# Attention with two passes over the scores: PSUM banks handled in units of two

## The reference

```python
h = _layernorm(x) * (1 + ca) + sa
q, k, v = split(h @ qkv_w + qkv_b)             # 16 heads of 8
q, k = _apply_rotary(q, rope), _apply_rotary(k, rope)
scores = einsum('bhqd,bhkd->bhqk', q, k) * 8 ** -0.5
scores = where(causal_mask, -inf, scores)
x = x + ga * (softmax(scores) @ v @ out_w + out_b)
h = _layernorm(x) * (1 + cb) + sb
x = x + gb * ffn(h)                            # routed expert: h = leaky(x @ w_fc) ** 2, h @ w_proj
```

## Time and profile before

| | |
|---|---|
| median of 3 runs | 369.53 us |
| the runs | 368.46 to 371.78 us |
| span of the profiled execution | 368.0 us |
| busy: TensorE, VectorE, ScalarE, GpSimd | 340.0, 258.0, 208.2, 103.8 us |

### The profile page before, as it was taken

How to read it: one execution, slowest core, us unless ns; L and a number is a source line. 1 busy time by engine, 2 the same in 40 slices (tenths; PEclk the granted TensorE clock), 3 DMA queues, 4 the chain that set the end, 5 groups by cost and what they waited for, 6 DMA issues and landing times.

```text
span 368.0 us, 6868 instructions
## 1 busy us (share of the span) xinstructions
PE 340.0 (92%) x2332; PEld 160.5 (44%) x2360; DVE 258.0 (70%) x563; ACT 208.2 (57%) x399; POOL 103.8 (28%) x189
## 2 busy tenths in 40 slices
PE   6999789999799898999999989999999999899886
PEld 4545345443354432443543434344434445434555
DVE  4947667987999977587667878677887777423254
ACT  5350056754166666677356665864666665785341
POOL 3543253427410424401301212101204232443221
PEclk9999889999999999999899999999999999999999
DMA  6547512221410003340230500500000000000000
GB/s 202 184 118 189 139 44 69 67 67 25 113 44 0 3 1 73 74 101 0 67 89 6 130 2 2 131 1 30 1 2 3 3 3 1 4 0 3 28 2 29
DMA packets 13314, 18.87 MB, mean 51 GB/s; under 512 B 4192, under 2 KB 9184, under 8 KB 13280
## 3 DMA queue, kind: packets, MB, share of 16 engines
q1 hardware_dynamic: 12992, 18.04, 18.4%
q10 hardware_dynamic: 288, 0.39, 0.3%
HBM read 12.98 MB, written 5.24 MB: 50 GB/s over the span
## 4 chain that ended last, share of the span: by engine, by line
PE 67%; issue 9%; DVE 8%; POOL 3%; ACT 2%; DMA 0%; SPq 0%; ACTq 0%; POOLq 0%; DVEq 0%
PE ps_o L1066 18%; PE ps L1029 15%; PE ps L1046 13%; PE ps L1000 4%; PE ps L987 4%; DVE tmax L864 3%; PE ps L936 3%; PE ps L1024 2%; DVE rot L760 1%; PE ps L1008 1%; PE ps L993 1%; PE ps L927 1%; PE ps L940 1%; ACT pt L660 1%; PE ps L947 1%
## 5 line engine op out<-in xcount | busy, mean ns | idle before, releaser
L864 DVE TENSOR_REDUCE tmax<-ps 128x1 f32<-128x512 f32 (+3 forms) x304 | 186.4, 656 | 65.4 <-PE ps L1029 65.0
L660 ACT ACTIVATE pt<-ps 128x512 f32<-128x512 f32 (+1 forms) x304 | 161.9, 576 | 105.6 <-PE ps L1046 104.1
L1029 PE MATMUL ps<-kst,qst 72*128 72x128 bf16 (+3 forms) x576 | 113.9, 274 | 3.6 <-issue 2.2
L1046 PE MATMUL ps<-qst,kst 75*128 75x512 bf16 (+3 forms) x384 | 111.0, 327 | 4.9 <-DVE rot L760 1.8
L1066 PE MATMUL ps_o<-pt,v_sb 128*32 128x512 f32 (+3 forms) x768 | 83.5, 507 | 2.0 <-ACT pt L660 1.1
L1029 PEld LDWEIGHTS ps<-kst,qst 72*128 72x128 bf16 x576 | 49.1, 98 | 70.0 <-ACT pt L660 17.9
L556 POOL TENSOR_SCALAR_AFFINE_SELECT pt<-pt 128x512 f32<-128x512 f32 x64 | 40.4, 641 | 68.0 <-ACT pt L660 67.5
L1046 PEld LDWEIGHTS ps<-qst,kst 75*128 75x128 bf16 x384 | 34.9, 98 | 29.6 <-issue 6.4
L1008 PE MATMUL ps<-maska,identb 128*128 128x512 bf16 x118 | 34.1, 396 | 3.5 <-POOL maska L483 3.3
L521 POOL CAST negp<-negm 128x16 bf16<-128x16 f32 x16 | 3.2, 198 | 94.4 <-DVE negm L781 94.2
L1066 PEld LDWEIGHTS ps_o<-pt,v_sb 128*32 128x32 f32 x768 | 15.5, 108 | 32.2 <-issue 17.3
(11 more groups left out here) (102 smaller groups left out, 250.8 us busy)
## 6 DMA issues: line engine op xcount, KB each, us to landing
qst<-qparts SPq DMA_DIRECT2D x48, 96.0 KB
kst<-kparts SPq DMA_DIRECT2D x48, 96.0 KB
qparts<-part SPq DMA_DIRECT2D x16, 96.0 KB, 1.9
kparts<-part SPq DMA_DIRECT2D x16, 96.0 KB, 1.9
xs<-in_x SPq DMA_DIRECT2D x4, 256.0 KB, 7.2
rope_sb<-in_rope SPq DMA_DIRECT2D x2, 512.0 KB, 6.2
qparts<-part SPq DMA_DIRECT2D x16, 64.0 KB, 1.8
qst<-negt SPq DMA_DIRECT2D x48, 4.0 KB, 1.7
```

The lines of the kernel that those rows point to most:

```text
L660: act.activation(pt[:, G % NP, h0:h0 + nh, 0:w], src, ACT.Exp, scale=SCALE).then_inc(s_exp, 1)
L864: dve.tensor_reduce(dst, src, AX.X, ALU.max).then_inc(s_max, 1)
L1029: last = pe.matmul(dst[:, j * nk:(j + 1) * nk], qst[0:ROWS, half, h, r * P:r * P + P], kst[0:ROWS, kh, h, k0:k0 + nk], start=(kind != "dia ...
L1046: last = pe.matmul(dst[:, j * w:(j + 1) * w], kst[:, kh, h, kt * P:kt * P + P], qst[:, half, h, c0:HALF], start=True, stop=True)
```

## The change

Pass A hands its banks over in units of up to two of one kind, and pass B in units of up to two of one group. Both diagonal blocks of two neighbouring rows make a unit (the second of them moves ahead of the tri and sq banks of its row), the tri block with a single bank stays alone, and so does a B group with one bank. A unit stands at the slot of its first bank and covers the following slot too. TensorE fills both its banks one after the other and signals once, after the last matmul. In a slot it now does the B unit first, then the A unit; `uses` has the same order. VectorE reduces, and ScalarE takes the exponential of, a whole unit in one instruction where its two banks are neighbours in the ring; where the ring ends between them (bank 6, then bank 0) there are two instructions. `bank_free` waits for the instruction that reads the bank in question. LEAD, PVLAG, NB and the stages' slots are as before.

```diff
-def bank_jobs_a(half):
+def bank_units_a(half):
+    units = []
     for r in range(TU):
-        jobs.append(("diag", r, 0, HG, P))
+        if r % 2 == 0:
+            units.append(("diag", [(r, 0), (r + 1, 0)], HG, P))
         if r:
             nh = min(HG, HALF // (r * P)) if r < 3 else 1
-            jobs += [("tri", r, h, nh, r * P) for h in range(0, HG, nh)]
+            banks = [(r, h) for h in range(0, HG, nh)]
+            units += [("tri", banks[j:j + 2], nh, r * P) for j in range(0, len(banks), 2)]
         if half:
-            jobs += [("sq", r, h, 1, HALF) for h in range(HG)]
+            units += [("sq", [(r, h), (r, h + 1)], 1, HALF) for h in range(0, HG, 2)]
...
+UNIT_B = 2
+NB = 7
...
         for gi, grp in enumerate(groups_b(half)):
-            for bank in grp[3]:
-                b_at[slot] = (s, gi, grp, bank, bank is grp[3][-1])
-                slot += 1
+            for j in range(0, len(grp[3]), UNIT_B):
+                unit = grp[3][j:j + UNIT_B]
+                b_at[slot] = (s, gi, grp, unit, unit[-1] is grp[3][-1])
+                slot += len(unit)
...
     for i in range(slots):
-        uses += [("a", i)] if i in a_at else []
-        uses += [("b", i)] if i in b_at else []
+        uses += [("b", (i, j)) for j in range(len(b_at[i][3]))] if i in b_at else []
+        uses += [("a", (i, j)) for j in range(len(a_at[i][1][1]))] if i in a_at else []
...
+    def operations(kind, i, n):
+        at = [use_no[(kind, (i, j))] % NB for j in range(n)]
+        return [(0, n)] if at == list(range(at[0], at[0] + n)) else [(j, 1) for j in range(n)]
...
             def exp(i):
-                act.wait_ge(s_b, n + 1)
+                act.wait_ge(s_b, unit_b[i] + 1)
...
-                src = bank_of("b", i)[:, 0:nh * w].rearrange("p (h q) -> p h q", h=nh)
-                act.activation(pt[:, G % NP, h0:h0 + nh, 0:w], src, ACT.Exp, scale=SCALE).then_inc(s_exp, 1)
+                for j, n in exp_ops[i]:
+                    h0, nh = unit[j]
+                    b0 = use_no[("b", (i, j))] % NB
+                    src = ps[:, b0:b0 + n, 0:nh * w].rearrange("p b (h q) -> p b h q", h=nh)
+                    dst = pt[:, G % NP, h0:h0 + n * nh, 0:w].rearrange("p (b h) q -> p b h q", b=n)
+                    act.activation(dst, src, ACT.Exp, scale=SCALE).then_inc(s_exp, 1)
...
-                    dve.wait_ge(s_a, i + 1)
+                    dve.wait_ge(s_a, unit_a[i] + 1)
...
+                    for j, n in max_ops[i]:
+                        r, h0 = banks[j]
+                        b0 = use_no[("a", (i, j))] % NB
+                        src = ps[:, b0:b0 + n, 0:nh * nk].rearrange("p b (h k) -> p b h k", h=nh)
...
+                        dve.tensor_reduce(dst, src, AX.X, ALU.max).then_inc(s_max, 1)
...
                 if kind == "a":
-                    pe.wait_ge(s_max, which + 1)
+                    pe.wait_ge(s_max, n_max[which])
                 if kind == "b":
-                    pe.wait_ge(s_exp, bank_no[which] + 1)
+                    pe.wait_ge(s_exp, n_exp[which])
...
+                for n, (r, h0) in enumerate(banks):
+                    dst = take("a", (i, n))
...
                 last.then_inc(s_a, 1)
...
             for i in range(slots):
+                if i in b_at:
+                    pass_b(i)
                 if i in a_at:
                     pass_a(i)
-                if i in b_at:
-                    pass_b(i)
-                if i not in b_at and i < max(a_at):
+                if i not in b_slots and i < a_end[-1] - 1:
                     keep_warm(1)
```

More of the change, by code:

```diff
@@ L122, in plan @@
     for s, (b, half, g) in enumerate(STEPS):
-        for job in bank_jobs_a(half):
-            a_at[n] = (s, job)
-            n += 1
+        for unit in bank_units_a(half):
+            a_at[n] = (s, unit)
+            n += len(unit[1])
         a_end.append(n)
@@ L186, in plan @@
                     at = put(at, name, (b, half, piece))
-    slots = max(list(a_at) + list(b_at) + list(v_at) + list(stages)) + 1
+    slots = max(a_end[-1:] + list(b_at) + list(v_at) + list(stages)) + 1
     return slots, a_at, b_at, v_at, stages, a_end
@@ L202, in adaln_block @@
         group_no.setdefault(b_at[i][0:2], len(group_no))
-    bank_no = {i: n for n, i in enumerate(sorted(b_at))}
+    unit_a = {i: n for n, i in enumerate(sorted(a_at))}
+    unit_b = {i: n for n, i in enumerate(sorted(b_at))}
+    b_slots = {i + j for i in b_at for j in range(len(b_at[i][3]))}
     prep_no = {u: n for n, u in enumerate(PREPS)}
@@ L294, in adaln_block @@
         y = sb("y", [P, TU, D])
-        NB = 7
         ps = bank("ps", NB)
@@ L1016, in pass_a @@
             def pass_a(i):
-                s, (kind, r, h0, nh, nk) = a_at[i]
+                s, (kind, banks, nh, nk) = a_at[i]
                 b, half, g = STEPS[s]
-                if i == 0 or a_at[i - 1][0] != s:
+                if i == 0 or a_end[s - 1] == i:
                     stack_ready(s)
-                dst = take("a", i)
-                if kind == "diag":
-                    pe.matmul(dst, identb[:, :], maska[:, :, :].rearrange("p h k -> p (h k)"), start=True, stop=False,
-                              skip_group_check=True)
@@ L1026, in pass_a @@
-                for j in range(nh):
-                    h = HG * g + h0 + j
-                    k0, kh = (r * P, half) if kind == "diag" else (0, half) if kind == "tri" else (0, 0)
-                    last = pe.matmul(dst[:, j * nk:(j + 1) * nk], qst[0:ROWS, half, h, r * P:r * P + P],
-                                     kst[0:ROWS, kh, h, k0:k0 + nk], start=(kind != "diag"), stop=True,
-                                     skip_group_check=True)
+                for n, (r, h0) in enumerate(banks):
+                    dst = take("a", (i, n))
+                    if kind == "diag":
+                        pe.matmul(dst, identb[:, :], maska[:, :, :].rearrange("p h k -> p (h k)"), start=True, stop=False,
+                                  skip_group_check=True)
+                    for j in range(nh):
+                        h = HG * g + h0 + j
+                        k0, kh = (r * P, half) if kind == "diag" else (0, half) if kind == "tri" else (0, 0)
+                        last = pe.matmul(dst[:, j * nk:(j + 1) * nk], qst[0:ROWS, half, h, r * P:r * P + P],
+                                         kst[0:ROWS, kh, h, k0:k0 + nk], start=(kind != "diag"), stop=True,
+                                         skip_group_check=True)
@@ L1042, in pass_b @@
                     pe.wait_ge(s_mstack[s % 2], 48 * (s // 2 + 1))
-                dst = take("b", i)
-                for j in range(nh):
-                    h = HG * g + h0 + j
-                    last = pe.matmul(dst[:, j * w:(j + 1) * w], kst[:, kh, h, kt * P:kt * P + P],
-                                     qst[:, half, h, c0:HALF], start=True, stop=True)
+                for n, (h0, nh) in enumerate(unit):
+                    dst = take("b", (i, n))
+                    for j in range(nh):
+                        h = HG * g + h0 + j
+                        last = pe.matmul(dst[:, j * w:(j + 1) * w], kst[:, kh, h, kt * P:kt * P + P],
+                                         qst[:, half, h, c0:HALF], start=True, stop=True)
@@ L1088, in _ @@
                     run(st)
-                    if i > max(b_at) and st[0] in WARM_POST:
+                    if i > max(b_slots) and st[0] in WARM_POST:
                         if st[0] == "n3" or st[1] == last_piece(len(UNITS) - 1):
```

45 lines of the change are left out of this document (28 added, 17 removed).

## The result

The changed kernel takes 397.99 us (median of 4 runs, 397.90 to 398.58) against 370.65 us (368.46 to 373.67) of the kernel before: a ratio of 1.076, interval [1.072, 1.0801], slower by 27 us. The forecast was 377 us and a range of 365 to 387. The direction came out, the size did not.

The account below looks back on a forecast made before the run. TensorE was taken to set the pace outside crowded stretches. Holes of 10.9 us, less 1.1 and 1.0, plus 0.3, gave 9.1, taken as 8; added to 369.5 this made 377.5, stated as 377 us, range 365 to 387.

Parts of the forecast that it names:

- The merged operations: Merged reductions on VectorE and exponentials on ScalarE: 8.4 and 11.6 us less busy time, 1.0 us counted on the path.
- The holes of the ring: TensorE waits 0.38 us before the V product for a bank that a merged reduction frees late.
- the list: Slots 79 to 303, where both passes run: 33 places short of TensorE work, 10.9 us together.
- net term: Holes of 10.9 us, less 1.1 and 1.0 for the crowded stretch, plus 0.3 in the tail: 9.1 us.
- the last part of the sum: VectorE's and ScalarE's other work ahead of awaited units, left out: 33 places at 0.2 more would be 6.6 us.
- Other parts: TensorE's instructions unchanged in number and size, B before A only reorders banks; 0.3 us in the tail, bounds 0 and 1.
- Slots before 79 at nothing: Single-pass slots before 79 counted as costing nothing, covered by a warming matmul per slot or the V product.
- a lost cover: Before slot 79, if warming matmuls or V products no longer cover the waits: up to 4.7 us.
- The clock: A drop of the granted clock, 1.00 in the quiet stretches, would spoil the reckoning upward; no size given.
- Piled-up holes: Rival, 386 us, chance 0.13: VectorE's stages ahead of merged reductions make 33 holes grow by 0.2 to 0.4 us.
- Balance: Rival, 370 us, chance 0.23: half the holes or less are new, 3 to 5 us, met by readers' savings of 3.
- faster: Rival, 364 us, chance 0.17: VectorE bounds more than one stretch, 5 to 6 of its saved 8.4 us come through.

Follow-up runs that it names:

- e17: Changed kernel's TensorE order, banks signalled one by one, merged reads moved to the slot of the unit's last bank, behind the first slot's stages; 376.74 us.
- e10: Changed kernel's TensorE order, but every bank signalled and read by itself at its own slot, nothing merged; 371.70 us.
- e14: Changed kernel with ten filling matmuls ahead of the first B unit and nine ahead of the first transposition of the maxima; 396.57 us.
- e6: Changed kernel with ten filling matmuls ahead of the first B unit; 397.41 us.
- e9: Kernel before with ten and five filling matmuls ahead of the first two transpositions of the maxima; 370.93 us.
- e15: Kernel before with ten filling matmuls ahead of the first transposition of the maxima and ten ahead of the first B bank; 370.69 us.

## Why the prediction was wrong, point by point

**The merged operations** were right: 1,220 and 1,023 ns against 1,215 and 1,018, and 120 and 129 fewer of them. VectorE's busy time fell by 6.2 us and ScalarE's by 11.4, for 8.4 and 11.6. None of it reached the end of the run. The Trainium skill (Perfetto Trace Analysis, section Optimizing Scalar/DVE Operations) says that instructions may better be broken up where Scalar and Vector are not saturated but make bubbles elsewhere; e17 against e10 agrees, 7.1 us longer in the middle for fewer operations.

**The holes of the ring** were right in place and mechanism, 0.40 for 0.38 us, and nearly so in number: e17 has 24 places and 8.4 us in the middle where the list had 33 and 10.9 us over a somewhat longer stretch; 6 of the 24, with 1.9 us, stand in e10 too. Their net term, 9.1 us, measured 7.1 in the middle of e17 and some 5 us in its whole time over e10.

**The step that failed** is the last part of the sum: "What VectorE's and ScalarE's other work adds when it stands ahead of a unit that TensorE waits for is not in it". First, it was left out of the sum, with 6.6 us as the most. Second, only one direction was seen, a stage that makes a unit late. The other direction decided: a unit that stands ahead of a stage makes the stage late by its wait for the second bank and its longer read, 0.75 us at the place shown, and TensorE waits for the stage's bank. Between the changed kernel and e17, which differ in this, in GpSimd's mask at the last bank's slot, and in the units that the ring splits (e17 signals and reads them bank by bank), lie 398.0 - 376.7 = 21 us. Some of that goes with the clock; with it nearly equal, e14 against e17 (8.2 and 2.2 us at 1.2 GHz there), the steps 0 to 12 differ by 60.2 + 214.9 - 53.9 - 204.5 = 16.7 us. In "Other parts" the sentence that the order B before A "only changes whose bank comes first" holds for TensorE (e10, 0.9987); the readers' order, which the diff changes with it, was not walked through with their stages.

**Slots before 79 at nothing** failed too. The steps 0 to 4 grew by 10.4 us. At nearly full clock (e14) they still take 60.2 us, and 53.9 in e17. At 61.61 us above, TensorE waits 1.72 us for `v_sb`, a stage again; the up to 4.7 us that the prediction named for a lost cover were for the ring.

**The clock** was named as what would spoil it upward. It did fall, and accounts for some 4 to 7 of the 27 us by the executions of e6 and e14; 4.9 us of it stand in the steps 0 to 4.

**The rivals.** Piled-up holes (386 us) was the nearest in kind, since it had stages and units in one queue; it had them the wrong way round. Balance and faster did not occur: VectorE was not the bound.

## What to carry to other kernels

Where an engine reads for another through one in-order queue, grouping two reads moves everything behind them later: walk through that queue with its other work before counting what the grouping saves, and ask who waits for that work. If reads are grouped, put the group where its last input comes, behind the small work that does not need it; here this turned 398 us into 377 with the same operations, some 17 of the 21 us at nearly the same clock. No version was measurably faster than the kernel before: bank by bank was the best of the grains tried here, where the readers have idle time.

## What was not expected of the hardware

The same time at the low clock did not cost the same everywhere. In the middle of the kernel before 3.4 us at 1.2 GHz cost 1.7 us (201.9 against 200.2 in e9 and e15), half of themselves; in the steps 0 to 4 of the changed kernel 15.1 us fewer brought only 4.9 (e14). And TensorE's clock followed the kernel's pauses, but not one by one: with the pauses filled that lie ahead of the low stretches at 41.4 and 51.6 us in the kernel before, the clock was low for 3.4 us each from 47.7 and 102.3 on instead (e9's profile), so a profile at one place does not tell what a fill is worth.
